# Four cross-attention layers on one core: probabilities transposed in two row tiles of 64 rows, two units a step, and the residual kept with features on the rows

## The chip, the cores and the metric

The kernel runs on one NeuronCore of a Trainium2 chip, one program with one launch. The metric is the device time of an execution in microseconds, the median of several runs. The profile is one further execution, recorded instruction by instruction. PE is TensorE (its weight loads are listed apart as PEld), DVE is VectorE, ACT is ScalarE, POOL is GpSimd, SP is SyncE, which issues the DMAs.

## What is computed

A batch of 128 sequences of 64 tokens with 128 features goes through four cross-attention layers against one context of 128 x 64 tokens with 256 features. Everything is float32. Layer 0 has 16 heads of width 64, a bias on some score columns, and a bias `bo`; layers 1 to 3 have an RMS norm ahead of the queries, 16 query heads and 4 key heads of width 8.

```python
# layer 0
q = x @ Wq;  k = ctx @ Wk;  v = ctx @ Wv            # 16 heads of 64
probs = softmax(q k^T / 8 + col_bias)
x = (probs v) @ Wo + bo + x
# layers 1, 2, 3
xn = x * rsqrt(mean(x*x) + eps) * norm_w
q = xn @ wq;  k = cond @ wk;  v = cond @ wv         # 16 query heads, 4 key heads of 8
x = x + (softmax(q k^T / sqrt(8)) v) @ wo
```

## The kernel before

The 128 sequences are cut into 32 groups g of four (T = 256 tokens). For every group the same list of *steps* is done, each named by kind, group, layer l and number u. On PE they are:

- `k` (4 steps, L694), `v` (6, L706), `k3` (L713): keys and values of all layers from the context; `q0` (4, L721): queries of layer 0.
- `s`: scores, in tiles of the PE array: layer 0 in tiles of 64 rows x 64 columns (L732), layers 1 to 3 in tiles of 32 rows x 64 columns (L743).
- `t` (L753): the probabilities of a *unit* transposed. A unit is an array `E` of 128 x 512: two sequences of 64 tokens on the 128 rows, eight heads of 64 keys along them. Each layer of a group has 4 units. One `t` step transposes one unit in four whole 128x128 pieces.
- `pv0` (L762, tiles of 64x64) and `pv` (L790, tiles of 128 rows x 32 columns): probabilities times values. `wo0` (L771) and `wo` (L796): output projection. `xt` (L665): the residual, kept with tokens on the rows (`xN`), is transposed to features on the rows (`xT`), from which `q` (L777) makes the queries of layers 1 to 3.

The softmax of a unit goes round the other engines: DVE takes the maximum and subtracts it (L954 and L958; layer 0 adds the bias and POOL subtracts), ACT exponentiates (L859, L852), DVE sums and inverts (L963, L966), POOL normalizes (L644), PE transposes, and ACT copies the result from PSUM back over `E` (`et`, L863). ACT also copies every other result of PE out of PSUM; DVE adds `wo0` and `wo` to the residual. PE results go through four PSUM banks in turn (`bank0` to `bank3`), the scores through four more. A step on PE waits until the previous user of its bank has been copied out.

The order of the steps on each engine is fixed by tables: each step has a time within a group's life, group g is moved by g x `PERIOD`, and every engine's queue is these times sorted. All engines wait for each other through semaphores. Four groups are thus under way at a time, in different layers. The last groups (28 to 31) have times of their own (`PE_ENDS` and so on), and the last two (`SPLIT`) do the steps of layers 1 to 3 and `wo0` in two halves of 128 tokens. `PE_FILL` puts 16 to 18 waits that are always fulfilled ahead of each `k` step on PE.

Of the kernel before, what the change touches and what calls it, by code (L numbers as in the profile page):

```python
# [40 lines left out]
PE_FILL = (18, 18, 16, 16)  # L41
PERIOD = 43.53
PE_TIME = {
    "k": {0: (30.28, 0, 14.31, 51.16)},
    "v": {0: (21.14, 37.8, 49.25, 36.09, 39.27, 41.84)},
    "k3": {0: (47.45,)},
    "q0": {0: (71.65, 69.92, 72.95, 66.36)},
    "s": {0: (76.07, 77.05), 1: (111.9,), 2: (143.36,), 3: (175.94,)},
    "t": {0: (94.04, 91.9, 96.41, 97.28),
          1: (130.16, 128.46, 122.67, 127.59),  # L50
          2: (159.58, 162.6, 158.28, 157.84),
          3: (194.83, 194.17, 193.73, 187.94)},
    "pv0": {0: (97.82, 98.8)},
    "wo0": {0: (103.09,)},
    "xt": {1: (107.55,), 2: (138.01,), 3: (169.65,)},
    "q": {1: (109.46,), 2: (140.38,), 3: (171.56,)},
    "pv": {1: (133.46,), 2: (165.14,), 3: (197.91,)},
    "wo": {1: (135.86,), 2: (167.94,), 3: (200.01,)},
}
ACT_TIME = {  # L60
    "k": {0: (34.56, 4.3, 18.1, 53.08)},
    "v": {0: (25.22, 39.25, 50.7, 37.55, 40.73, 44.78)},
    "k3": {0: (49.49,)},
    "q0": {0: (74.13, 70.98, 74.63, 70.11)},
    "exp": {0: (80.41, 85.19, 87.75, 85.75),
            1: (120.19, 118.66, 116.45, 120.9),
            2: (152.96, 153.95, 147.98, 149.19),
            3: (188.52, 182.87, 185.84, 180.45)},
    "et": {0: (95.03, 92.53, 97.11, 97.91),
           1: (130.79, 130.12, 123.35, 128.23),  # L70
           2: (160.7, 163.23, 159.03, 158.54),
           3: (195.63, 194.86, 194.37, 189.23)},
    "pv0": {0: (99.49, 100.47)},
    "x2": {1: (109.06,), 2: (141.94,), 3: (169.29,)},
    "xt": {1: (108.29,), 2: (139.06,), 3: (170.23,)},
    "q": {1: (110.14,), 2: (141.13,), 3: (173.37,)},
    "pv": {1: (134.61,), 2: (166.3,), 3: (199.06,)},
}
DVE_TIME = {
    "add": {0: (77.25, 81.06, 83.78, 79.49)},  # L80
    "max": {0: (78.14, 82.16, 84.55, 80.38),
            1: (113.05, 115.01, 114.34, 117.07),
            2: (145.86, 148.79, 144.51, 145.18),
            3: (181.14, 177.77, 182.49, 177.09)},
    "sum": {0: (86.87, 85.92, 88.83, 87.95),
            1: (126.36, 120, 117.74, 122.34),
            2: (153.84, 154.84, 149.47, 151.71),
            3: (190.07, 183.75, 186.72, 181.81)},
    "rcp": {0: (88.63, 86.67, 92.27, 92.07),
            1: (127.12, 121.47, 119.11, 123.71),  # L90
            2: (154.59, 157.26, 151.51, 153.54),
            3: (191.43, 185.32, 187.47, 184.43)},
    "wo0": {0: (106.87,)},
    "ssq": {1: (109.6,), 2: (142.68,), 3: (174.61,)},
    "sub": {1: (118.42, 116.38, 115.69, 119.31),
            2: (150.82, 152.38, 147.21, 148.1),
            3: (185.52, 180.45, 184.63, 178.44)},
    "wo": {1: (136.51,), 2: (168.81,), 3: (200.99,)},
}
POOL_TIME = {  # L100
    "xb": {0: (33.37,)},
    "sub": {0: (79.26, 82.91, 85.3, 81.5)},
    "nrm": {0: (89.03, 86.94, 92.55, 93.59),
            1: (127.48, 121.74, 119.39, 123.99),
            2: (155.66, 157.53, 151.78, 154.61),
            3: (191.71, 187.69, 188.74, 184.7)},
    "ms": {1: (110.08,), 2: (143.16,), 3: (175.09,)},
}
SP_TIME = {
    "cT": {0: (116.06,)},  # L110
    "kr": {1: (50.03,), 2: (73.03,), 3: (104.56,)},
    "lt": {0: (127.56,)},
    "xT": {0: (128.06,)},
    "st": {0: (202.62,)},
}

PE_ENDS = {
    28: {  # L120
        "s": {3: (172.75,)},
        "t": {2: (159.47, 159.47, 158.28, 157.84), 3: (187.48, 189.3, 186.49, 186.58)},
        "xt": {3: (168.97,)},
        "q": {3: (169.89,)},
        "pv": {2: (164.38,), 3: (190.31,)},
        "wo": {2: (164.61,), 3: (191.31,)},
    },
    29: {
        "s": {2: (142.53,), 3: (171.37,)},
        "t": {1: (128.31, 131.24, 129.24, 125.42),  # L130
              2: (159.07, 155.87, 157.44, 155.61),
              3: (218.3, 187.25, 190.66, 197.07)},
        "xt": {2: (135.25,), 3: (166.95,)},
        "q": {2: (137.77,), 3: (168.74,)},
        "pv": {1: (131.42,), 2: (163.31,), 3: (219.88,)},
        "wo": {1: (133.21,), 2: (165.67,), 3: (224.77,)},
    },
# [13 lines left out]
    },  # L151
# [891 lines left out]
```

## Time and profile before

| | |
|---|---|
| Runs | 1444.02, 1445.4, 1445.58 us; median 1445.4 |
| Span of the profiled execution | 1442.6 us (the runs are 1.4 to 3.0 us above it) |
| PE busy | 1416.4 us (98%), weight loads 1151.5 us |
| DVE, ACT, POOL busy | 1090.9, 1043.0, 787.3 us |
| Granted TensorE clock | full (2.4 GHz) in nearly every stretch |
| HBM | 20.68 MB read, 4.19 MB written |

A "busy" PE is one that has a matmul somewhere in its pipeline, so 98% says that it never stops, not that it streams data all the time. How long a step takes is therefore read from the start of one step to the start of the next. In the rows, `x4` counts machine instructions: a float32 matmul is two of them, a transpose is one.

### The profile page before, as it was taken

The numbers are of one execution on the slowest core, as the hardware profiler recorded it, in microseconds if no ns is written. First come the engines' busy times: TensorE is split into PE (matmuls) and PEld (weight loads), VectorE is DVE, ScalarE is ACT, GpSimd is POOL, SyncE is SP. The second block draws the span as 40 slices with busy tenths as digits, with TensorE's granted clock in tenths as the row PEclk, the third lists the DMA queues.
The fourth block names the chain that finished last, engine by engine and source line by source line (L and its number), as shares of the span: only waits on it lengthen the run. The fifth ranks groups of instructions, "written<-read, shape, count | busy, mean of one in ns | idle before, by whom it ended". The sixth has DMA issues, their size and how long they took to land.

```text
span 1442.6 us, 56878 instructions
## 1 busy us (share of the span) xinstructions
PE 1416.4 (98%) x23692; PEld 1151.5 (80%) x23692; DVE 1090.9 (76%) x2281; ACT 1043.0 (72%) x2321; POOL 787.3 (55%) x905
## 2 busy tenths in 40 slices
PE   8999999999999999999999999999999999999987
PEld 6778878888888888788888788888888887888765
DVE  1557777777777777777778777777777777777887
ACT  3567776777777777767777777777777777677777
POOL 3445555545555455555455555455554555554687
PEclk9999999999999999999999999999999999999999
DMA  5010111010111001111001110101110001110000
GB/s 157 21 28 18 29 29 30 24 29 18 30 29 31 23 18 29 30 29 30 24 19 29 29 30 24 29 19 29 29 32 23 23 25 30 29 28 18 18 7 14
DMA packets 58540, 41.16 MB, mean 29 GB/s; under 512 B 17456, under 2 KB 54064, under 8 KB 58288
## 3 DMA queue, kind: packets, MB, share of 16 engines
q1 hardware_dynamic: 57872, 37.19, 9.9%
q8 instruction: 192, 3.15, 0.9%
q14 instruction: 60, 0.49, 0.1%
q10 hardware_dynamic: 416, 0.33, 0.1%
HBM read 20.68 MB, written 4.19 MB: 17 GB/s over the span
## 4 chain that ended last, share of the span: by engine, by line
PE 96%; ACT 1%; DVE 1%; POOL 1%; issue 1%; DMA 0%
PE bank L706 17%; PE bank L694 16%; PE bank L753 16%; PE bank L771 8%; PE bank L721 7%; PE scores L743 7%; PE bank L790 7%; PE scores L732 5%; PE bank L762 5%; PE bank L796 3%; PE bank L777 3%; PE bank L713 2%; PE bank L665 1%; ACT E L863 1%; DVE st L954 0%
## 5 line engine op out<-in xcount | busy, mean ns | idle before, releaser
L644 POOL TENSOR_TENSOR E<-E,st 128x512 f32<-128x512 f32 x512 | 530.2, 1044 | 535.7 <-DVE st L966 535.5
L963 DVE TENSOR_REDUCE st<-E 128x8 f32<-128x512 f32 x512 | 344.7, 675 | 81.0 <-ACT E L859 40.0
L863 ACT COPY E<-bank 128x512 f32<-128x512 f32 x512 | 298.1, 598 | 96.7 <-PE bank L753 95.5
L859 ACT ACTIVATE E<-E,inv 128x512 f32<-128x512 f32 x384 | 278.5, 734 | 57.2 <-DVE E L958 56.7
L954 DVE TENSOR_REDUCE st<-scores 128x8 f32<-128x512 f32 x372 | 244.0, 683 | 97.0 <-PE scores L743 97.0
L753 PE MATMUL bank<-ident,E 128*128 128x128 f32 x2048 | 301.5, 276 | 0.9 <-POOL E L644 0.7
L753 PEld LDWEIGHTS bank<-ident,E 128*128 128x128 f32 x2048 | 241.5, 141 | 69.3 <-issue 28.2
L706 PE MATMUL bank<-wv,cT 128*128 128x374 f32 (+1 forms) x768 | 271.4, 478 | 0.0
L694 PE MATMUL bank<-cT,wk 128*128 128x256 f32 x1024 | 245.9, 384 | 7.0 <-issue 5.9
L958 DVE TENSOR_TENSOR E<-scores,st 128x512 f32<-128x512 f32 x372 | 245.9, 669 | 0.1
L694 PEld LDWEIGHTS bank<-cT,wk 128*128 128x128 f32 x1024 | 188.9, 192 | 32.1 <-issue 6.3
L706 PEld LDWEIGHTS bank<-wv,cT 128*128 128x128 f32 x768 | 132.1, 191 | 49.8
L640 POOL TENSOR_TENSOR E<-E,st 128x512 f32<-128x512 f32 x140 | 146.1, 1044 | 29.8 <-DVE st L948 26.0
L721 PE MATMUL bank<-xq,wq 128*128 128x256 f32 x512 | 131.0, 380 | 0.0
L820 ACT COPY V<-bank 128x374 f32<-128x374 f32 (+1 forms) x192 | 85.1, 443 | 50.7 <-PE bank L706 46.6
L771 PEld LDWEIGHTS bank<-wo,QT 128*128 128x128 f32 x1024 | 119.4, 192 | 2.1 <-ACT QT L868 0.3
L771 PE MATMUL bank<-wo,QT 128*128 128x128 f32 x1024 | 119.9, 275 | 0.1
L941 DVE TENSOR_TENSOR E<-scores,bias 128x512 f32<-128x512 f32 x128 | 86.2, 674 | 40.8 <-PE scores L732 40.8
L790 PEld LDWEIGHTS bank<-E,VB 128*32 128x32 f32 x6144 | 90.6, 110 | 28.6 <-issue 22.2
L743 PE MATMUL scores<-KB,QT 32*64 32x256 f32 x3072 | 110.1, 389 | 2.4 <-DVE E L958 1.5
L895 ACT COPY QT<-bank 128x256 f32<-128x256 f32 (+1 forms) x102 | 36.7, 360 | 102.0 <-PE bank L790 98.1
L790 PE MATMUL bank<-E,VB 128*32 128x64 f32 x6144 | 106.9, 221 | 3.2 <-ACT E L863 3.1
(58 smaller groups left out, 1627.0 us busy)
## 6 DMA issues: line engine op xcount, KB each, us to landing
KB<-K SPq DMA_DIRECT2D x1536, 8.0 KB
cT<-in_ctx_t SPq DMA_DIRECT2D x32, 256.0 KB, 2.8
xq<-in_x_t SPq DMA_DIRECT2D x32, 128.0 KB, 2.2
xin<-in_x SPq DMA_DIRECT2D x32, 128.0 KB, 2.3
out<-xN SPq DMA_DIRECT2D x30, 128.0 KB, 1.9
wk<-in_L_xattn_Wk SPq DMA_DIRECT2D x3, 256.0 KB, 5.5
wv<-in_L_xattn_Wv SPq DMA_DIRECT2D x2, 374.0 KB, 6.4
wq<-in_L_xattn_Wq SPq DMA_DIRECT2D x1, 512.0 KB, 6.2
```

The lines of the kernel that those rows point to most:

```text
L644: e.tensor_tensor(E3, E3, wide(stat[s][u][:, 16:24]), ALU.mult).then_inc(g_nrm.sem, 1)
L694: m = e.matmul(bank[:, T * jj:T * jj + T], wk0[:, k, 128 * j:128 * j + 128], cTg[:, k, :], start=(k == 0), stop=(k == 1))
L706: m = e.matmul(bank[:, 0:hi - lo], cTg[:, k, 128 * p:128 * p + 128], wv[:, k, lo:hi], start=(k == 0), stop=(k == 1))
L721: m = e.matmul(bank[:, T * jj:T * jj + T], wq0[:, 128 * j:128 * j + 128], xq[g % NX][:, :], start=True, stop=True)
L753: m = e.transpose(bank[:, 128 * k:128 * k + 128], E[s][u][:, 128 * k:128 * k + 128], ident[:, :])
L771: m = e.matmul(bank[:, 128 * p:128 * p + 128], QT[s][:, j, 128 * p:128 * p + 128], wo0[:, j, :], start=(j == 0), stop=(j == 7))
L790: m = e.matmul(bank[32 * r:32 * r + 32, 64 * b:64 * b + 64], VBg[:, b, c:c + 32], E[s][2 * (b // 2) + r // 2][:, n:n + 64], start=(gp == 0 ...
L859: e.activation(E[s][u][:, :], E[s][u][:, :], ACT.Exp, scale=inv[s][:, u // 2:u // 2 + 1]).then_inc(a_exp.sem, 1)
L863: e.copy(E[s][u][:, :], bank_of["t", g, l, u][:, :]).then_inc(a_et.sem, 1)
L954: e.tensor_reduce(stat[s][u][:, 0:8].rearrange("p (r h) -> p r h", r=2), scores_of[g, l, u], AX, ALU.max).then_inc(d_max.sem, 1)
L958: e.tensor_tensor(pairs(E[s][u][:, :]), scores_of[g, l, u], stat[s][u][:, 0:8].rearrange("p (r h a) -> p r h a", r=2, a=1).to_broadcast([1 ...
L963: e.tensor_reduce(stat[s][u][:, 8:16], heads(E[s][u][:, :]), AX, ALU.add).then_inc(d_sum.sem, 1)
```

## The change

**The transposes.** A `t` step now does two units (u = 0 or 1 stands for units 2u and 2u+1) and takes two banks. Each piece is the 64 rows of one sequence by 128 columns of `E` (two heads), transposed against a 64x64 identity into a 128x64 result. The upper and lower 64 rows go in turn, the upper to the first bank and the lower to the second, which is how the PE array is used as two row tiles. A unit was four instructions of 128 moving columns; it is eight of 64. `et` copies a whole bank as before; what lies where in `E` afterwards is different, and `pv0` and `pv` read it from there, with the same count of matmuls in the same tiles.

**The residual.** It is kept as `xT`, features on the rows. `wo0` and `wo` have the weights as the stationary operand and the 256 tokens as the moving one (half as many instructions of twice the columns). `xq`, the transposed input that `q0` reads, is also the residual's start: DVE adds `bo` (one number per row) and `xq` in one operation. `xN`, `xin`, their loads, the `bo` addition on POOL (`xb`), the `xt` transposes and their ACT copies are gone. The sum of squares needs tokens on the rows, so a step `x2` transposes `xT` (same size as `xt`), and ACT squares it out of PSUM. The output is stored transposed and turned back on the host; the next load of `xq` waits for `wo0`.

**The order.** All tables are new, `PERIOD` is 41.50 instead of 43.53, the tables of the last groups are empty, `SPLIT` is empty, `PE_FILL` is zero.

```diff
-PE_FILL = (18, 18, 16, 16)
-PERIOD = 43.53
+PE_FILL = (0, 0, 0, 0)
+PERIOD = 41.500813
...
-SPLIT = range(NG - 2, NG)
+SPLIT = range(NG, NG)
...
-            at = [(n + i) % 4 for i in range(2 if st[0] == "pv0" else 1)]
+            at = [(n + i) % 4 for i in range(2 if st[0] in ("pv0", "t") else 1)]
...
+                    w.wait_ge(d_ev, *[("wo0", g, 0, part(g, p)) for p in range(NP)])
                     e.dma_start(xq[g % NX][:, :], t["x_t"][g + NX]).then_inc(l_xq[g % NX].sem, 16)
...
-                    w.wait_ge(g_nrm, ("nrm", g, l, u))
-                    for k in range(4):
-                        m = e.transpose(bank[:, 128 * k:128 * k + 128], E[s][u][:, 128 * k:128 * k + 128], ident[:, :])
+                    w.wait_ge(g_nrm, ("nrm", g, l, 2 * u), ("nrm", g, l, 2 * u + 1))
+                    for r in range(2):
+                        for k in range(4):
+                            for i in range(2):
+                                rows, n = slice(64 * i, 64 * i + 64), 256 * r + 64 * k
+                                m = e.transpose(bank[i][:, n:n + 64], E[s][2 * u + r][rows, 128 * k:128 * k + 128],
+                                                ident[rows, rows])
                     m.then_inc(p_t.sem, 1)
...
-                    for p in halves(g, u):
-                        for j in range(8):
-                            m = e.matmul(bank[:, 128 * p:128 * p + 128], QT[s][:, j, 128 * p:128 * p + 128],
-                                         wo0[:, j, :], start=(j == 0), stop=(j == 7))
+                    for j in range(8):
+                        m = e.matmul(bank[:, tokens], wo0[:, j, :], QT[s][:, j, tokens], start=(j == 0), stop=(j == 7))
...
-                elif kind == "xt":
+                elif kind == "x2":
+                    w.wait_ge(l_ident, "ident")
                     w.wait_ge(d_ev, ("wo0" if l == 1 else "wo", g, l - 1, u))
                     for p in halves(g, u):
-                        to_rows(bank, 128 * p, xN[s][:, p, :], p == halves(g, u)[-1])
+                        m = e.transpose(bank[:, 128 * p:128 * p + 128], xT[s][:, 128 * p:128 * p + 128], ident[:, :])
+                    m.then_inc(p_ev.sem, 1)
...
                 elif kind == "et":
-                    w.wait_ge(p_t, ("t", g, l, u))
-                    e.copy(E[s][u][:, :], bank_of["t", g, l, u][:, :]).then_inc(a_et.sem, 1)
+                    w.wait_ge(p_t, ("t", g, l, u // 2))
+                    e.copy(E[s][u][:, :], bank_of["t", g, l, u // 2][u % 2][:, :]).then_inc(a_et.sem, 1)
...
-                    e.tensor_tensor(flat(xN[s])[:, tokens], bank[:, tokens], flat(xin[s])[:, tokens], ALU.add
-                                    ).then_inc(d_ev.sem, 1)
+                    e.scalar_tensor_tensor(xT[s][:, tokens], bank[:, tokens], bo[:, 0:1], xq[g % NX][:, tokens], ALU.add,
+                                           ALU.add).then_inc(d_ev.sem, 1)
```

What this does to PE's queue is seen at two places of a period in the middle of the program. The first is the stretch from the scores of layer 1 to the scores of layer 0. Before (`wos` is the weight of `wo`, `E_3` the fourth unit):

```order
L743 MATMUL scores<-KB_0,QT 64x256 x16
L796 MATMUL bank<-wos,QT 128x128 x2
L721 MATMUL bank<-xq,wq 128x256 x2
L753 MATMUL bank<-ident,E_3 128x128 x4
L753 MATMUL bank<-ident,E_2 128x128 x4
L721 MATMUL bank<-xq,wq 128x256 x2
L753 MATMUL bank<-ident,E_0 128x128 x4
L721 MATMUL bank<-xq,wq 128x256 x2
L694 MATMUL bank<-cT,wk 128x256 x4
L753 MATMUL bank<-ident,E_1 128x128 x4
L732 MATMUL scores<-KT,QT 64x64 x64
```

and now, at the same place (L476 are the scores of layer 1, L454 is `q0`, L427 `k`, L439 `v`, L489 `t`, L465 the scores of layer 0):

```order
L476 MATMUL scores<-KB_1,QT 64x256 x16
L454 MATMUL bank<-xq,wq 128x256 x2
L532 MATMUL bank<-QT,wos 128x256
L427 MATMUL bank<-cT,wk 128x256 x4
L454 MATMUL bank<-xq,wq 128x256 x6
L489 MATMUL bank<-ident,E_0 128x64 x8
L489 MATMUL bank<-ident,E_1 128x64 x8
L439 MATMUL bank<-wv,cT 128x374 x2
L489 MATMUL bank<-ident,E_2 128x64 x8
L489 MATMUL bank<-ident,E_3 128x64 x8
L465 MATMUL scores<-KT,QT 64x64 x64
```

The four transposes stood singly between whole-array matmuls, themselves whole-array work; now they stand in two pairs, each in the two-row-tile form, with a whole-array `v` between them. The second place is the end of a period, from the scores of layer 2 over `wo0` to the `q` of layer 1. Before:

```order
L743 MATMUL scores<-KB_1,QT 64x256 x16
L753 MATMUL bank<-ident,E_3 128x128 x4
L694 MATMUL bank<-cT,wk 128x256 x4
L771 MATMUL bank<-wo,QT 128x128 x16
L753 MATMUL bank<-ident,E_2 128x128 x4
L753 MATMUL bank<-ident,E_1 128x128 x4
L665 MATMUL bank<-ident,xN 128x128 x2
L753 MATMUL bank<-ident,E_0 128x128 x4
L706 MATMUL bank<-wv,cT 128x374 x2
L777 MATMUL bank<-xT,wqs 128x256
```

and now (L507 is `wo0`, L512 `q`, L518 the new `x2`):

```order
L476 MATMUL scores<-KB_1,QT 64x256 x16
L489 MATMUL bank<-ident,E_2 128x64 x8
L489 MATMUL bank<-ident,E_3 128x64 x8
L507 MATMUL bank<-QT,wo 128x256 x8
L489 MATMUL bank<-ident,E_0 128x64 x8
L489 MATMUL bank<-ident,E_1 128x64 x8
L439 MATMUL bank<-wv,cT 128x374 x2
L512 MATMUL bank<-xT,wqs 128x256
L518 MATMUL bank<-ident,xT 128x128 x2
```

The `k` step between the `pv0` steps and `wo0` is gone from there, `wo0` is enclosed by two transposing pairs, and `q` no longer waits for a transpose and its copy.

## Rows read from the trace of the kernel before

**Rows 1.** The page, busy time of each engine and share of the span.

```profile
PE 1416.4 (98%) x23692; PEld 1151.5 (80%) x23692; DVE 1090.9 (76%) x2281; ACT 1043.0 (72%) x2321; POOL 787.3 (55%) x905
```

**Rows 2.** The page, the chain that ended last, by engine.

```profile
PE 96%; ACT 1%; DVE 1%; POOL 1%; issue 1%; DMA 0%
```

**Rows 3.** Timeline of PE, the `wo0` steps of groups 3, 18, 29 and 31.

```profile
176.95 3.73 PE L771 MATMUL bank<-wo,QT 128*128 128x128 f32 x32
...
834.19 3.73 PE L771 MATMUL bank<-wo,QT 128*128 128x128 f32 x32
...
1316.17 3.73 PE L771 MATMUL bank<-wo,QT 128*128 128x128 f32 x32
...
1384.87 1.95 PE L771 MATMUL bank<-wo,QT 128*128 128x128 f32 x16
```

**Rows 4.** Busy time by windows: 14 periods, and the end.

```profile
220.80:834.20 613.40, 612.69 (x10362) 501.09 (x10361) 478.92 (x995) 450.22 (x994) 333.12 (x378) 1.00 0.10 27
...
1384.90:1442.60 57.70, 44.87 (x836) 33.19 (x834) 44.84 (x102) 46.21 (x116) 43.75 (x56) 0.97 0.04 12
```

Columns: window, its length, then busy us and instructions of PE, PEld, DVE, ACT, POOL, then granted clock, DMA share and GB/s.

**Rows 5.** Timeline of PE in a middle period: start, length, line, operation, array tile, count.

```profile
804.67 1.89 PE L694 MATMUL bank<-cT,wk 128*128 128x256 f32 x8
806.40 0.60 PE L753 MATMUL bank<-ident,E 128*128 128x128 f32 x4
806.93 2.10 PE L732 MATMUL scores<-KT,QT 64*64 64x64 f32 x128
808.96 1.10 PE L790 MATMUL bank<-E,VB 128*32 128x64 f32 x64
809.99 0.66 PE L753 MATMUL bank<-ident,E 128*128 128x128 f32 x4
810.48 1.42 PE L706 MATMUL bank<-wv,cT 128*128 128x374 f32 x4
...
817.92 1.89 PE L694 MATMUL bank<-cT,wk 128*128 128x256 f32 x8
819.74 1.12 PE L743 MATMUL scores<-KB,QT 32*64 32x256 f32 x32
820.79 1.10 PE L790 MATMUL bank<-E,VB 128*32 128x64 f32 x64
821.82 1.10 PE L713 MATMUL bank<-cT,wks 128*96 128x256 f32 x4
822.76 0.60 PE L753 MATMUL bank<-ident,E 128*128 128x128 f32 x4
823.20 0.61 PE L796 MATMUL bank<-wos,QT 128*128 128x128 f32 x4
```

**Rows 6.** Weight loads of tile `bank` by line: ns min/median/max, first and last start.

```profile
L790 PEld LDWEIGHTS bank<-E,VB x6144: 106/110/110, 77.2 to 1438.1; 128*32 128x32 f32 x199
L762 PEld LDWEIGHTS bank<-E,V x4096: 129/135/135, 48.0 to 1387.6; 64*64 64x64 f32 x196
L753 PEld LDWEIGHTS bank<-ident,E x2048: 137/141/230, 43.0 to 1436.5; 128*128 128x128 f32 x187
L694 PEld LDWEIGHTS bank<-cT,wk x1024: 186/190/337, 5.9 to 1365.4; 128*128 128x128 f32 x171
```

**Rows 7.** The page, costliest groups: busy us, mean ns of one, idle before.

```profile
L644 POOL TENSOR_TENSOR E<-E,st 128x512 f32<-128x512 f32 x512 | 530.2, 1044 | 535.7 <-DVE st L966 535.5
...
L753 PE MATMUL bank<-ident,E 128*128 128x128 f32 x2048 | 301.5, 276 | 0.9 <-POOL E L644 0.7
L863 ACT COPY E<-bank 128x512 f32<-128x512 f32 x512 | 298.1, 598 | 96.7 <-PE bank L753 95.5
...
L790 PE MATMUL bank<-E,VB 128*32 128x64 f32 x6144 | 106.9, 221 | 3.2 <-ACT E L863 3.1
```

**Rows 8.** Timeline of PE, the step ahead of the first `wo0`.

```profile
50.56 1.97 PE L694 MATMUL bank<-cT,wk 128*128 128x256 f32 x8 [0.46 <-ACT QT L868]
```

More of the change, by code:

```diff
@@ L73 @@
[L73 to L77, printed above, removed]
+    "k": {0: (3.68386, -15.27201, -6.17337, 31.67261)},
+    "v": {0: (1.38578, 7.02085, 22.92723, 7.72795, 7.45838, 19.83981)},
+    "k3": {0: (20.92541,)},
+    "q0": {0: (46.49501, 45.92059, 43.6006, 46.83102)},
+    "exp": {0: (53.45354, 53.85427, 64.05064, 60.19724),
+            1: (89.26426, 87.38091, 88.31216, 89.8139),
+            2: (119.0247, 119.99253, 120.41612, 125.81305),
+            3: (157.12044, 158.35286, 146.78456, 148.29428)},
@@ L78 @@
+    "et": {0: (72.80188, 70.12283, 74.38432, 74.91003),
+           1: (94.37576, 97.20368, 92.87151, 93.63442),
+           2: (130.02138, 130.69038, 130.95683, 130.76886),
+           3: (163.36371, 165.90794, 161.03983, 161.0276)},
+    "pv0": {0: (77.48236, 77.47354)},
+    "x2": {1: (84.45866,), 2: (118.43633,), 3: (137.54581,)},
+    "q": {1: (83.49375,), 2: (115.56548,), 3: (133.12088,)},
+    "pv": {1: (104.57246,), 2: (131.76498,), 3: (167.77863,)},
 }
 DVE_TIME = {
-    "add": {0: (77.25, 81.06, 83.78, 79.49)},
@@ L81 @@
[L81 to L98, printed above, removed]
+    "add": {0: (55.2541, 53.04177, 57.80328, 56.50077)},
+    "max": {0: (55.53031, 55.83358, 59.00545, 58.41666),
+            1: (87.28643, 84.47971, 84.43642, 89.53838),
+            2: (118.07358, 118.40023, 119.44369, 120.23959),
+            3: (152.51299, 148.31429, 145.74995, 142.83961)},
@@ new lines @@
+    "sum": {0: (60.32318, 64.11482, 68.19706, 64.69957),
+            1: (93.38689, 90.42387, 92.61554, 94.70716),
+            2: (123.99953, 123.33926, 124.87226, 125.45511),
+            3: (155.08859, 158.66318, 155.26501, 154.11835)},
+    "rcp": {0: (61.15165, 64.66232, 68.84377, 65.42065),
+            1: (94.25659, 92.98835, 94.45288, 95.94984),
+            2: (125.00317, 124.44888, 125.29739, 126.52991),
+            3: (156.56917, 160.68649, 158.46443, 154.92969)},
+    "wo0": {0: (81.3189,)},
@@ L360 @@
-SPLIT = range(NG - 2, NG)
-ON_ACT = ("q0", "pv0", "xt", "q", "pv", "k", "v", "k3")
+}
+SPLIT = range(NG, NG)
+ON_ACT = ("q0", "pv0", "x2", "q", "pv", "k", "v", "k3")
 ON_DVE = ("wo0", "wo")
@@ L505, in xattn_kernel @@
         for st in of(PE_ORDER, *ON_ACT, *ON_DVE, "t"):
-            at = [(n + i) % 4 for i in range(2 if st[0] == "pv0" else 1)]
+            at = [(n + i) % 4 for i in range(2 if st[0] in ("pv0", "t") else 1)]
             n += len(at)
             before[st] = [held[i] for i in at if held[i]]
-            bank_of[st] = [banks[i] for i in at] if st[0] == "pv0" else banks[at[0]]
-            for i in at:
-                held[i] = st
+            bank_of[st] = [banks[i] for i in at] if st[0] in ("pv0", "t") else banks[at[0]]
+            for j, i in enumerate(at):
+                held[i] = ("et", *st[1:3], 2 * st[3] + j) if st[0] == "t" else st
         l_ident = signal("l_ident", ["ident"], 16)
@@ L591, in sync_program @@
                 s = g % NS
-                if kind == "xT" and g + NS < NG:
-                    w.wait_ge(d_ev, ("wo0", g, 0, 0))
-                    e.dma_start(xin[s][:, :, :], x_r[g + NS]).then_inc(l_x[s].sem, 16)
-                elif kind == "cT" and g + NC < NG:
+                tokens = slice(128 * halves(g, u)[0], 128 * halves(g, u)[-1] + 128)
+                if kind == "cT" and g + NC < NG:
                     w.wait_ge(p_ev, ("k3", g, 0, 0), *[("k", g, 0, i) for i in range(4)], *[("v", g, 0, i) for i in range(6)])
@@ L794, in tensor_program @@
                     w.wait_ge(a_ev, ("pv", g, l, u))
-                    for p in halves(g, u):
-                        m = e.matmul(bank[:, 128 * p:128 * p + 128], QT[s][:, 1, 128 * p:128 * p + 128],
-                                     wos[:, l - 1, :], start=True, stop=True)
+                    m = e.matmul(bank[:, tokens], wos[:, l - 1, :], QT[s][:, 1, tokens], start=True, stop=True)
                     m.then_inc(p_ev.sem, 1)
```

326 lines of the change are left out of this document (53 added, 273 removed), and 55 rows, old and new, of tables (ACT_ENDS, PE_ENDS).

## The prediction, made before the changed kernel ran

> **What bounds the kernel now.** I read the busy times first: PE 98%, its weight loads 80%, DVE 76% [rows 1]. Then the chain that ended last: 96% of it is PE [rows 2]. Then the places of `wo0`, to see the rhythm: group 3 at 176.95, group 18 at 834.19, so 657.24 / 15 = 43.82 us a group; group 29 at 1316.17 is 26 such periods after group 3 to within 0.1 [rows 3]. In 14 of these periods PE is busy 612.69 of 613.40 us, DVE 478.92, that is 34.2 a period [rows 4]. So the span is 177 of start, 26 periods that PE's queue sets, and 126.4 from group 29's `wo0` to the end. A step's price is its share of PE's queue: start to start.
>
> **What a step costs on PE** [rows 5]. `k`, 8 instructions of 256 columns, takes 1.73 (804.67 to 806.40): 0.216 each. `t` takes 0.44 (822.76 to 823.20): 0.110 for 128 columns. `wo0`, 32 of 128 columns, would by this be 3.5; it stands at about 3.6 with its tail (length 3.73, [rows 3]). Tiled steps work in rounds, one matmul in each tile. Layer-0 scores: 128 in four tiles, 32 rounds, 2.03. `pv`: 64 in four tiles, 16 rounds, 1.03. The matmul's own length falls from 276 for 128 columns to 221 for 64 [rows 7], 0.86 ns a column, so a round of 64 columns streams 0.055; 16 of them are 0.88 and 32 are 1.76. The rest, 0.15 and 0.27, is the price of changing the shape of the array, plus a few ns a round.
>
> Three readings isolate that price. `k` ahead of scores takes 1.82 (817.92 to 819.74) instead of 1.73: **0.09** on leaving. A first whole-array step after tiled work is longer: `k3` 0.94 (821.82 to 822.76) instead of 4 x 0.216, **0.08**; `t` 0.49 (809.99 to 810.48) instead of 0.44, **0.05**. That second part goes with the first weight load, which nothing hides: loads last 110 for 32 columns, 135 for 64, 190 for 128, about 0.85 ns a column, but only 141 for the 128 columns of a transpose [rows 6], some 0.055 of streaming against 0.109. So entering a whole-array matmul costs 0.09 + 0.10 or so, 0.20 with rounding up; entering a transpose 0.09 + 0.055, 0.15.
>
> **The change, per period.**
>
> *The transposes.* 64 instructions x 0.110 = 7.0 become 128 of 64 columns in two tiles, 64 rounds. No row has this form. The lower bound of a round is the streaming 0.055, as in `pv`; the layer-0 scores (2.03 / 32 = 0.063 with their change of shape in it, about 0.058 without) are the nearest with two row tiles. I take 0.056: 3.6. **-3.4**. The upper bound is that the tiles do not overlap, 0.110 a round, no gain at all.
>
> *Changes of shape.* Before, a period had 12; the transposes were whole-array work like their neighbours. Now they are a shape of their own. From the order: seven blocks of them (t3.0, t2.0, t2.1, t1, t0.0, t0.1, t3.1; only layer 1's pairs stand together), so 7 x 0.15 = 1.05 to enter; and the whole array is entered nine times (eight matmuls, one `x2`: 8 x 0.20 + 0.15 = 1.75) instead of four (`wo`, `k3` and two `t`: 0.20 + 0.17 + 2 x 0.15 = 0.67). The eight entries to scores, `pv` and `pv0` stay. **+2.1**. Bounds: 0, if two row tiles switch for nothing, and 12 x 0.20 = 2.4.
>
> *wo0 and wo.* 16 x 0.216 = 3.46 for about 3.57, and 3 x 0.43 for 3 x 0.44. **-0.1**. *xt to x2*: same matmuls, 0. *The fills*: PE has no idle time that they could explain in the middle [rows 4]; 0, at most 0.2 gained.
>
> Sum -3.4 + 2.1 - 0.1 = **-1.4 us**: a period of 42.4.
>
> Two rules of the Trainium skill bear on this; the sum above does without them. TensorEngine Tiling (Properties) says that changing the tiling mode, not just the tile, drains the engine; the trace agrees, with 0.09 on each change. TensorE: Matmul & The Clock Gate (LDWEIGHTS) gives a weight load as columns / 1.2 ns whatever the number of rows. It speaks against this change: 64 rows do not halve the load, a round would be limited by a 128-column load of 107 ns, and by the page the transposes would still cost 64 x 0.107 = 6.8. The trace's plain loads agree with it in slope; the transposes' load is shorter by 0.05 [rows 6], so I side with the row.
>
> **What hides the rest.** DVE needs 34.2 of the 42.4 us, 81% [rows 4]; the 1.1 us less of copies on ACT and the POOL addition are off the path and give nothing. `wo0` waits for two `pv0` steps' copies, four of about 0.64, 2.6 from the first's end; it is covered by the second `pv0` (1.0), scores (1.05 and a change) and a pair of transposes (0.6), so just. If that cover is short, PE loses tenths a period. A `t` now waits for two units normalized instead of one, 1.044 on POOL later [rows 7], and fills two of the four banks in 0.6 where ACT needs 2 x 0.598 to empty them [rows 7]. Mostly 1.3 to 1.7 of whole-array work stands behind it, so I price this at 0 and keep it as a rival. The later load of `xq` has two periods to land: 0. SP's queue stands behind that wait, but its next entries are due later: 0.
>
> **Start and end.** Start: half-filled periods save some 2 us up to group 3; the first `wo0` had `k` ahead of it and still waited 0.46 for the copy [rows 8], and without it waits some 1.7 more. Together 0; within 2.
>
> End: without the split, each layer of the last group is one serial chain. From group 29's `wo0`: (a) one period without the `k` of group 32, 42.4 - 1.7 = 40.7. (b) The next has no `k`, `v`, `k3`: PE would need 27, but DVE still has four softmaxes, 34.2. Each hangs in a chain, so I take 37. (c) From group 31's `wo0`, five and a half layers of softmax at 34.2 / 4 = 8.55, 47 of DVE; then two places where nothing else is left to fill: between layers 2 and 3 of group 31, and behind the last. From the last inverse: one or two normalizations at 1.044, `t` 0.6, two `et` 1.2, `pv` 1.1, copy 0.4, `wo` 0.6, add 0.4, `q` 0.6, copy 0.4, scores 1.1, about 7.5. Twice that is 15, and the start of this stretch and the store 4: 66. Sum 143.7 instead of 126.4: **+17**. Before, this last stretch took 57.7 with PE busy only 44.87 and DVE 44.84 of it [rows 4]. I give the sum 8 either way.
>
> **Sum.** 177 + 26 x 42.4 + 143.7 = 1423.1, say 1423.5 against the profiled 1442.6: -19. The profiled execution's span lies 2.8 under the median 1445.4; with that carried over, **1426 us**, 1.3% faster.
>
> **Rivals.**
>
> 1. *The forecast*: rounds overlap, changes of shape eat 60% of the gain. 1410 to 1442. 0.50.
> 2. *Changes of shape are cheap for two row tiles* (a whole-height array split in two might not drain). For: `k3`, 96 columns, changes shape for nothing. Against: every other tiled step pays 0.09 [rows 5]. Without them a period is 40.3, 28 periods x 2.1 less: 1367; with half, 1396. 0.24.
> 3. *The change doesn't do what it says*: two row tiles do not overlap, because the 128-column load sets the pace. For: the number of loads doubles and each is as wide as before; no row shows two such loads side by side. Against: `pv0` and scores in 64x64 tiles load and stream in two row tiles at once. T stays at 7.0, the period becomes 45.8: 1426 + 29 x 3.4 = 1525. Slower than before once a round takes over 0.085. 0.12.
> 4. *Banks and pairs*: transposes overlap, but PE waits at its seven blocks for ACT to empty two banks, or for the second unit. Where an `et` is late by one copy, 0.6, at three of the seven, that is 1.8 a period x 26: 1473. It decides against the change from 0.75 us a period. For: ACT already waits for PE rather than the reverse [rows 7], so there is slack; against it, PE's steps got shorter and the copies did not. 0.10.
>
> 0.04 is left for a mixture that ends within 0.2% (3 us, what a measurement of this kernel can tell from no change). Range for 8 in 10: all of 1, the upper half of 2, the lower part of 4: 1386 to 1452. Faster: 0.50 + 0.24 + a part of 4, less the tail of 1: 0.78. Same 0.04, slower 0.18.
>
> **What would show it.** Between two `wo0` in the middle 42.4 us. A pair `t` to the next step 0.6 (0.45 of rounds, 0.15 to enter), against 0.5 if rival 2 holds and 1.0 if 3 does; the next `v` longer than 1.26 + 0.09 by 0.1. PE's idle before `t` and `wo0` still near nothing; if ACT's `et` stands there with over 0.5 us a period, rival 4. DVE at some 81% in the middle. From group 29's `wo0` to the end 144. The forecast is wrong if the round isn't 0.056, if the change of shape has another price for this tile, or if the end, for which there is no row of an unsplit group alone, takes over 155.

## The result and the profile after

The changed kernel takes **1469.8 us** (median of 4 runs, 1464.1 to 1472.4) against 1444.7 for the kernel before (4 runs): ratio 1.0169, interval 1.0146 to 1.0193. It is slower, by 1.7%; 1426 was forecast, and the range ended at 1452. The profiled execution took 1467.5, with a span of 1465.7.

The page of the changed kernel, span and busy time of each engine, beside [rows 1]:

```profile
span 1465.7 us, 58100 instructions
...
PE 1395.2 (95%) x25024; PEld 1064.8 (73%) x25024; DVE 1088.6 (74%) x2291; ACT 998.0 (68%) x2177; POOL 748.9 (51%) x849
```

PE is busy 21 us less than before in a span that is 23 us longer: 44 us more of idle time have come in. Where they lie is seen by windows: a stretch of the middle as long as fourteen periods, and two stretches at the end (columns as in [rows 4]).

```profile
220.00:834.00 614.00, 601.87 (x10948) 460.57 (x10948) 474.00 (x995) 434.29 (x953) 322.92 (x365) 1.00 0.09 24
1310.60:1392.80 82.20, 70.67 (x1490) 53.85 (x1488) 67.17 (x143) 55.01 (x115) 46.01 (x52) 0.96 0.08 18
1392.80:1465.70 72.90, 42.48 (x736) 29.74 (x732) 42.41 (x92) 30.55 (x58) 24.80 (x29) 0.63 0.03 9
```

In the middle PE is idle 12 of 614 us, where it was idle 0.7 of 613 [rows 4]; in the last 73 us it is idle 30, at a mean granted clock of 0.63. The timeline gives the rhythm, again by the places of `wo0` (now L507), first four in the middle (groups 18 to 21), then those of groups 29 to 31:

```profile
832.33 3.72 PE L507 MATMUL bank<-QT,wo 128*128 128x256 f32 x16
875.58 3.72 PE L507 MATMUL bank<-QT,wo 128*128 128x256 f32 x16
919.12 3.72 PE L507 MATMUL bank<-QT,wo 128*128 128x256 f32 x16
961.66 3.72 PE L507 MATMUL bank<-QT,wo 128*128 128x256 f32 x16
...
1310.56 3.72 PE L507 MATMUL bank<-QT,wo 128*128 128x256 f32 x16
1354.59 3.72 PE L507 MATMUL bank<-QT,wo 128*128 128x256 f32 x16
1392.84 3.72 PE L507 MATMUL bank<-QT,wo 128*128 128x256 f32 x16
```

The periods are 43.25, 43.54, 42.54: the last comes within 0.14 of the forecast 42.4, but they are not alike, while before all were 43.8 [rows 3]. Group 3's `wo0` stands at 175.4, so 26 periods took 1310.56 - 175.4 = 1135.2, 43.66 on the mean. Against before: the start -1.5 us, the middle -4 (forecast -37), the end 155.1 instead of 126.4, +28.7 (forecast +17). -1.5 - 4 + 28.7 = 23, the difference of the spans.

What PE waited for, by total (columns: the line that waited, what ended the wait, us in total, times, the longest), for the changed kernel:

```profile
PE bank L489 <- POOL E L383: 17.7, 9, 8.9
PE bank L527 <- issue: 12.4, 14, 1.3
...
PE scores L476 <- issue: 4.7, 9, 1.3
PE scores L465 <- issue: 4.1, 8, 0.8
```

The first row lies in the end of the program, but for 0.3. The three with "issue", 21.2 us together, are idle time for which the profile shows nothing to wait for, and they stand *inside* a step. The timeline of PE shows one:

```profile
801.21 0.71 PE L489 MATMUL bank<-ident,E 64*128 64x64 f32 x16
801.85 1.52 PE L439 MATMUL bank<-wv,cT 128*128 128x374 f32 x4
803.31 0.71 PE L489 MATMUL bank<-ident,E 64*128 64x64 f32 x16
803.94 2.10 PE L465 MATMUL scores<-KT,QT 64*64 64x64 f32 x128
805.97 0.65 PE L527 MATMUL bank<-E,VB 128*32 128x64 f32 x30
807.95 0.72 PE L527 MATMUL bank<-E,VB 128*32 128x64 f32 x34 [1.34 <-issue]
```

`pv` halts for 1.34 us after 30 of its 64 matmuls, though all its inputs are there. Counting PE's instructions in the trace (weight loads, matmuls, semaphore waits) from the first, each such halt in the middle stands behind number 192 or 193 modulo 256. The places 256 instructions apart are called *limits* of the blocks below. And among the DMA queues of the page there is one that carries instructions (packets, MB, share); here it is for the changed kernel, and for the kernel before:

```profile
q8 instruction: 197, 3.23, 0.9%
```

```profile
q8 instruction: 192, 3.15, 0.9%
```

3.23 MB in 197 packets are 16.4 KB each, and PE's 2 x 25024 loads and matmuls with some 500 waits, divided by 197, are about 256 to a packet. Hence the theory: **PE's instructions arrive in blocks of 256, and a block that is used up too fast leaves PE waiting for the next.** The layer-0 scores use 256 instructions in 2.03 us, and `pv` of layer 2 another 128 in 1.03 right behind them.
The records of the single packets tie the two together. The halt above ends 1.3 us after a packet of that queue has landed, and so does every other: the 136 halts of over 0.4 us between 170 and 1440 us in the changed kernel and in four of the kernels below (b_nofill, b_shift, h_bad, f_whole) all stand at a limit, and each ends 1.2 to 1.6 us after a packet landed, with a median of 1.4; of all times in h_bad, only some 6% lie that far behind a landing. A packet takes 0.9 to 1.5 us.

The Trainium skill describes the mechanism (Runtime: NRT & Kernel Launch, Instruction fetch mechanics): a FIFO for each engine that is refilled in blocks of 256 instructions over a DMA queue of its own; the 16.4 KB packets of some 256 instructions agree. The Trainium skill adds there that the fetch is hidden since the sequencer issues slower than blocks arrive; the halts measured here, 0.4 to 1.3 us each in the changed kernel, say that this doesn't hold for PE with small tiled matmuls.

### The profile page after: what moved, and what is told of

Same layout as the page of the kernel before. It is cut to its first block, busy times and chain, and to the rows that moved or that the text cites. A ratio compares the mean times of both kernels' runs of the same rounds, so it can differ in the third digit from the quotient of the medians.

```text
span 1465.7 us, 58100 instructions
## 1 busy us (share of the span) xinstructions
PE 1395.2 (95%) x25024; PEld 1064.8 (73%) x25024; DVE 1088.6 (74%) x2291; ACT 998.0 (68%) x2177; POOL 748.9 (51%) x849
## 3 DMA queue, kind: packets, MB, share of 16 engines
q8 instruction: 197, 3.23, 0.9%
## 4 chain that ended last, share of the span: by engine, by line
PE 90%; DVE 3%; issue 2%; ACT 2%; POOL 1%; SPq 1%; DMA 0%; POOLq 0%; DVEq 0%; ACTq 0%
PE bank L439 17%; PE bank L427 15%; PE bank L489 11%; PE bank L454 8%; PE bank L507 7%; PE scores L476 7%; PE bank L527 7%; PE scores L465 5%; PE bank L499 4%; PE bank L532 3%; PE bank L512 3%; PE bank L446 2%; PE bank L518 2%; DVE st L680 1%; DVE E L684 1%
## 5 line engine op out<-in xcount | busy, mean ns | idle before, releaser
L383 POOL TENSOR_TENSOR E<-E,st 128x512 f32<-128x512 f32 x512 | 527.8, 1042 | 371.7 <-DVE st L692 369.4
L599 ACT COPY E<-bank 128x512 f32<-128x512 f32 x512 | 274.0, 589 | 29.1 <-PE bank L489 27.3
L439 PE MATMUL bank<-wv,cT 128*128 128x374 f32 (+1 forms) x768 | 283.9, 493 | 0.4 <-issue 0.4
L684 DVE TENSOR_TENSOR E<-scores,st 128x512 f32<-128x512 f32 x384 | 255.4, 679 | 2.2
L427 PE MATMUL bank<-cT,wk 128*128 128x256 f32 x1024 | 250.2, 388 | 4.7 <-DMA wk<-in_L_xattn_Wk 4.7
L489 PEld LDWEIGHTS bank<-ident,E 64*128 64x128 f32 x4096 | 150.7, 141 | 102.1 <-issue 70.6
L427 PEld LDWEIGHTS bank<-cT,wk 128*128 128x128 f32 x1024 | 191.2, 191 | 33.2 <-issue 4.6
L489 PE MATMUL bank<-ident,E 64*128 64x64 f32 x4096 | 182.0, 232 | 19.4 <-POOL E L383 17.7
L439 PEld LDWEIGHTS bank<-wv,cT 128*128 128x128 f32 x768 | 133.9, 189 | 61.0 <-issue 0.7
L379 POOL TENSOR_TENSOR E<-E,st 128x512 f32<-128x512 f32 x128 | 129.5, 1043 | 87.8 <-DVE st L674 87.8
L395 POOL TENSOR_TENSOR nt<-nt,powers 128x2 f32<-128x2 f32 x96 | 18.7, 195 | 240.5 <-DVE nt L711 240.5
L548 ACT COPY KT<-bank 128x512 f32<-128x512 f32 x128 | 75.0, 586 | 82.2 <-PE bank L427 82.2
L454 PE MATMUL bank<-xq,wq 128*128 128x256 f32 x512 | 124.2, 385 | 0.0
L476 PE MATMUL scores<-KB,QT 32*64 32x256 f32 x3072 | 115.5, 396 | 6.6 <-issue 4.7
L507 PE MATMUL bank<-QT,wo 128*128 128x256 f32 x512 | 119.0, 386 | 1.3 <-ACT QT L604 1.3
L580 ACT ACTIVATE QT<-bank 128x512 f32<-128x512 f32 x128 | 75.7, 592 | 61.3 <-PE bank L532 56.5
```

Of the source, the lines that this page charges most:

```text
L383: e.tensor_tensor(E3, E3, wide(stat[s][u][:, 16:24]), ALU.mult).then_inc(g_nrm.sem, 1)
L427: m = e.matmul(bank[:, T * jj:T * jj + T], wk0[:, k, 128 * j:128 * j + 128], cTg[:, k, :], start=(k == 0), stop=(k == 1))
L439: m = e.matmul(bank[:, 0:hi - lo], cTg[:, k, 128 * p:128 * p + 128], wv[:, k, lo:hi], start=(k == 0), stop=(k == 1))
L454: m = e.matmul(bank[:, T * jj:T * jj + T], wq0[:, 128 * j:128 * j + 128], xq[g % NX][:, :], start=True, stop=True)
L489: m = e.transpose(bank[i][:, n:n + 64], E[s][2 * u + r][rows, 128 * k:128 * k + 128], ident[rows, rows])
L507: m = e.matmul(bank[:, tokens], wo0[:, j, :], QT[s][:, j, tokens], start=(j == 0), stop=(j == 7))
```

## The experiments

Each kernel ran on one chip beside runs of the kernel before; times are medians, with the ratio to that kernel and its interval. Kernels from different chips are compared by these ratios.

**1. b_nofill: the kernel before without its fills.**

```diff
-PE_FILL = (18, 18, 16, 16)
+PE_FILL = (0, 0, 0, 0)
```

> The kernel before with PE_FILL set to (0, 0, 0, 0) and nothing else: 68 waits that are always met already go from each group, 34 of TensorE's instructions, so that a group has 1502 of them instead of 1536 = 6 x 256. Theory of the instruction blocks: TensorE's instructions come in blocks of 256, and a block that begins late in the long run of small matmuls of s of layer 0 and pv of layer 2 is not there in time; with 1502 a group the places where the blocks begin wander over the group, and now and then one falls there. Periods between 43.7 and 45, not constant, 0.5 to 1.2 us more a group on the mean, 1458 to 1475 us. Rival, the waits are padding without use: 1443 to 1447 us, periods constant at 43.8. Rival, they cost their 0.106 us an instruction: 3.6 us a group less, down to 1350 us.

1483.7 us, ratio 1.0279 (1.0247 to 1.0311). To take away 68 waits a group that never wait costs 40 us. The mean period is 45.35 and the single ones go from 43.75 to 48.2; those without a halt are 43.75, so the 34 instructions themselves cost 0.07 us. The effect is larger than the 1458 to 1475 expected. Six halts of 1.4 to 2.5 us, 11.8 in total, lie in `pv0`, while halts were expected in the layer-0 scores and `pv` alone:

```profile
309.62 0.68 PE L762 MATMUL bank<-E,V 64*64 64x64 f32 x28 [2.54 <-issue]
```

In these six the packet itself starts late: 1.8 to 6.1 us after the last limit, 1.0 to 1.8 us after `pv0` has begun; for the halts elsewhere in this kernel it is 0.2 to 1.7 us after the limit. PE goes on 1.2 to 1.5 us after it has landed, as everywhere. What makes a packet start late was not tested.

Both rivals fall.

**2. b_shift: the kernel before, its blocks moved.** Waits on a load that is long done, in the first three groups alone:

```diff
-                    for _ in range(PE_FILL[u]):
+                    for _ in range(PE_FILL[u] + (EARLY if g < 3 else 0)):
...
+                    for _ in range(V_FILL + (EARLY if g < 3 else 0)):
+                        e.wait_ge(l_wk[1].sem, 16)
```

with `EARLY = 7`, `V_FILL = 0`.

> The kernel before with 7 more met waits at each k and v step of the first three groups alone (some 105 instructions in the first 140 us, where TensorE waits for loads anyway), and nothing else. Every group after them is the same as before, with 1536 instructions. Theory of the instruction blocks: the blocks now begin at other places, one of them 337 instructions into the run of s of layer 0 and pv of layer 2 (it was 184 in, and the next after the run), in every group: each period 44.6 to 45.8 us instead of 43.82, all alike, 1465 to 1500 us. Rival, the place of an instruction in its block has no effect: periods 43.8, 1445 to 1452 us with what the waits at the start may cost.

1512.6 us, ratio 1.0473 (1.0455 to 1.049), the slowest kernel here and above the 1465 to 1500 expected, though from the fourth group on it is the kernel before, instruction for instruction. The mean period is 46.40 us. What PE waited for, by total:

```profile
PE bank L794 <- issue: 31.1, 28, 1.6
PE bank L696 <- issue: 16.8, 29, 6.0
PE bank L757 <- issue: 13.0, 22, 1.0
```

A halt of 1.1 in `pv` (L794) in each group was expected. That a group loses 2.6 us and not 0.8 to 2 has two reasons above all: another limit falls behind `pv0` and `s`, into a transpose (L757, up to 1.0, 13.0 in total), and the fills of the `k` step that follows (L696) now lie open, some 0.4 us each time, where before they hid behind queued matmuls. The three rows, without the one wait of 6.0, make 2.0 of the 2.6; the rest is not itemised.

**3. h_align and h_bad: the changed kernel, its blocks fixed in a good and in a bad place.** Three of the eight pairs are transposed on the whole array again, 16 instructions less each; with 4 for the fills a group has 1580 - 48 + 4 = 1536.

```diff
-PE_FILL = (0, 0, 0, 0)
+PE_FILL = (2, 2, 2, 2)
+EARLY = 9
...
+WHOLE = {(0, 1), (2, 0), (0, 0)}
...
+                            if (l, u) in WHOLE:
+                                m = e.transpose(bank[r][:, 128 * k:128 * k + 128],
+                                                E[s][2 * u + r][:, 128 * k:128 * k + 128], ident[:, :])
+                                continue
```

`pv0` and `pv` read E for these pairs where the kernel before has it. h_bad differs by `EARLY = 13` alone.

> The changed kernel with whole-array transposes for three of its eight transpose steps (both of layer 0 and the first pair of layer 2, those that stand alone between whole-array steps), two met waits at each k step and nine more at each k and v step of the first three groups: 1536 instructions a group, with the blocks' beginnings where the changed kernel was fastest (phase 136 of 256 at wo0). Theory of the instruction blocks: periods constant at 42.5 to 42.9 us with no issue idle inside pv, 1436 to 1448 us (26 times 1.0 less than the changed kernel's mean of 43.66; its end stays near 155 us). Rival, the row tiles themselves or contention make the long periods: they stay at 43.4 or more and vary, 1462 us or more.

> h_align with thirteen instead of nine extra waits at the k and v steps of the first three groups, and nothing else: the steady groups are the same instruction for instruction, at phase 196 of 256, so that a block begins 377 instructions into the run of s of layer 0 and pv of layer 2. Theory of the instruction blocks: periods constant at 43.8 to 45 us, 1470 to 1500 us. Rival, the row tiles or contention: the same as h_align within 3 us.

h_align: **1436.4** us, ratio 0.9941 (0.992 to 0.9962). h_bad: **1487.9**, ratio 1.0303 (1.0288 to 1.0319). One number, which acts in the first three groups alone, is worth 51 us. Both lie in the ranges of the theory. From group 2 to group 28 every period of h_align is 42.64 or 42.65; here are three of its `wo0`:

```profile
855.50 3.72 PE L519 MATMUL bank<-QT,wo 128*128 128x256 f32 x16
898.14 3.72 PE L519 MATMUL bank<-QT,wo 128*128 128x256 f32 x16
940.78 3.72 PE L519 MATMUL bank<-QT,wo 128*128 128x256 f32 x16
```

h_bad's run from 43.8 to 45.2, 44.55 on the mean; they were expected to be constant. The same place of the group in the timeline, h_align first:

```profile
787.28 2.10 PE L470 MATMUL scores<-KT,QT 64*64 64x64 f32 x128
789.30 1.10 PE L542 MATMUL bank<-E,VB 128*32 128x64 f32 x64
790.34 1.52 PE L444 MATMUL bank<-wv,cT 128*128 128x374 f32 x4
```

and h_bad:

```profile
819.02 2.10 PE L470 MATMUL scores<-KT,QT 64*64 64x64 f32 x128
821.05 1.09 PE L542 MATMUL bank<-E,VB 128*32 128x64 f32 x61
823.38 0.30 PE L542 MATMUL bank<-E,VB 128*32 128x64 f32 x3 [1.25 <-issue]
823.62 1.52 PE L444 MATMUL bank<-wv,cT 128*128 128x374 f32 x4
```

And what h_bad waited for, by total:

```profile
PE bank L542 <- issue: 30.5, 29, 1.7
...
PE bank L498 <- issue: 10.4, 24, 0.9
```

30.5 + 10.4 = 41 of the 51 us are named. The rest is not itemised, but the rows above show a part of it: from the `scores` to the `v` behind them h_bad takes 4.60 us and h_align 3.06, that is 1.54 more with a halt of 1.25, so 0.3 more comes in beside each such halt; the three matmuls behind the halt take 0.24 (823.38 to 823.62), where 64 of them take 1.04 otherwise. The packets fit: in h_bad one is under way from 820.82 to 821.94, and PE goes on at 823.38. Since the two kernels have the same steady instructions, the rival (tiles or contention) is out.

All blocks of the steady part of seven kernels (f_whole is experiment 4), worked out from the records: by the time in which PE used up a block, how many there are, and the median and largest gap at its end, in us.

```
block used in   < 2.3 us        2.3 to 2.8      2.8 to 3.5      3.5 to 5        > 5 us
before          -               -               -               -               169: 0.11 0.22
after           27: 0.92 1.55    5: 0.31 1.11    3: 0.31 0.86   13: 0.04 0.97   126: 0.04 0.41
h_align         -               -               -               -               169: 0.05 0.31
h_bad           29: 1.19 1.89   28: 0.58 1.13   -               -               113: 0.04 0.17
f_whole         28: 0.69 1.77   -               -                4: 0.21 0.21   126: 0.04 0.72
b_shift         56: 1.00 1.79   -               -               -               113: 0.03 0.04
b_nofill        22: 1.20 1.86    5: 0.31 1.86    4: 1.26 2.35    8: 0.26 2.15   126: 0.04 2.76
```

A block used in 2.0 us is followed by a gap of about 1, one used in 2.5 by 0.6, and above 5 there is hardly any but in b_nofill. So the next block takes about 3 us to come, as a rule: 0.8 or so until its packet starts, 1.1 for the packet, 1.4 until PE goes on. Where the packet starts later, as in the `pv0` of b_nofill, a block that was used more slowly is followed by a halt too.

**4. f_whole: all transposes on the whole array, nothing else undone.**

```diff
+WHOLE = {(0, 1), (2, 1), (0, 0), (3, 1), (1, 1), (2, 0), (3, 0), (1, 0)}
```

> The changed kernel with all eight transpose steps of a group on the whole array (the probabilities then lie in E as before, and pv0 and pv read them there); pairs of units, order, end and everything else as in the changed kernel. 1452 instructions a group, so the blocks' beginnings wander; the periods whose wo0 stands at 140 to 165 of 256 should be free of their waits and give the pure price. Theory that the row tiles pay only where tiled steps are neighbours: 43.5 to 43.8 us there, 1.0 to 1.2 above the changed kernel's best 42.54. Rival, the tiles save 0.24 us at each of 8 places (forecast of 32 columns of time less a step): 44.4 or more. Second rival, the changes of shape eat all of it: 42.6.

1488.7 us (one run). 1452 instructions a group; the blocks wander, the mean period is 44.57. The periods without a halt are 43.63 to 43.64, eight of them, as the theory had it; the rivals, 44.4 and 42.6, are out. Here is one:

```profile
800.18 3.62 PE L515 MATMUL bank<-QT,wo 128*128 128x256 f32 x16
843.82 3.62 PE L515 MATMUL bank<-QT,wo 128*128 128x256 f32 x16
```

So the row tiles are worth 43.63 - 42.54 = **1.09 us** a group. In h_align three pairs without them cost only 42.64 - 42.54 = 0.10 (with its four fills in it); the other five bring 0.99. A pair in row tiles takes 0.64 (801.21 to 801.85) and on the whole array 0.87:

```profile
803.64 1.04 PE L489 MATMUL bank<-ident,E 128*128 128x128 f32 x8
804.51 1.42 PE L440 MATMUL bank<-wv,cT 128*128 128x374 f32 x4
805.77 0.59 PE L520 MATMUL bank<-xT,wqs 128*128 128x256 f32 x2
```

but the `v` behind it takes 1.26 here (804.51 to 805.77) and 1.46 behind the tiled one (801.85 to 803.31). So a tiled pair that stands alone between whole-array steps gains 0.23 and loses 0.20 again; the 0.99 of the other five, 0.20 each, says that next to another tiled step a pair keeps most of its gain.

**5. b_nosplit: the kernel before with the end of the changed one.** `PE_ENDS` to `SP_ENDS` empty, and

```diff
-SPLIT = range(NG - 2, NG)
+SPLIT = range(NG, NG)
```

> The kernel before without its tables for the last groups (PE_ENDS to SP_ENDS empty) and without the split of the last two (SPLIT empty), nothing else; the groups up to wo0 of group 28 keep their order, their 1536 instructions and their blocks. Theory that the split and the tables of the last groups carried the end: from wo0 of group 29 to the end 148 to 158 us instead of 126.4, and with the three periods ahead of it unchanged 1466 to 1476 us. Rival, the longer end of the changed kernel is of its deeper order (124 us from wo0 to the last wo of a group, 97 before): then leaving out the split alone costs 3 to 10 us, 1448 to 1455 us.

1463.8 us, ratio 1.0138 (1.0121 to 1.0155). `wo0` of group 29 stands at 1316.4, the span ends at 1460.9: 144.5 instead of 126.4. That is +18, somewhat under the 148 to 158 of the first theory and far over the rival. So of the +28.7 us at the changed kernel's end, some 18 come from the split and the tables of the last groups, if these are worth as much there as in the kernel before.

**6. h_warm: matmuls on constants where PE idles in the last two groups.**

```diff
+                warm = {"t": 3, "pv": 3, "wo": 1, "q": 1}.get(kind, 0) if g >= 30 and l else 0
+                if kind == "t" and warm:
+                    first = [x for x in PE_ORDER if x[:3] == (kind, g, l)][0]
+                    warm = 0 if st != first else 18 if (g, l) == (31, 3) else 3
+                for _ in range(warm):
+                    e.matmul((bank[0] if kind == "t" else bank)[:, 0:256], wo0[:, 0, :], wk0[:, 0, 0:256],
+                             start=True, stop=True)
```

> h_align, with matmuls of 256 columns on constants (their result is overwritten) where TensorE waits for its input in the layers 1 to 3 of the last two groups: 3 ahead of the first t and of pv of each layer, 1 ahead of q and wo, 18 ahead of the first t of the last layer; 0.43 us each at full clock, about what TensorE idles there. Theory that the granted clock of half speed lengthens the end: the clock stays at 1.0 to the end, the steps of the chain that took 1.9 to 2.0 us at half clock (s, pv) take 1.1, and the end of 147.4 us from wo0 of group 29 falls by 4 to 7 us, 1429 to 1433. Rival, the end is the chain of VectorE, ScalarE and GpSimd, and the added work is in the way: no change or up to 5 us more.

1433.8 us, ratio 0.9934 (0.9917 to 0.995): not to be told from h_align's 0.9941, though the theory expected 1429 to 1433. The last rows of PE in h_align, at the lower of the two clock levels (granted 0.50 there):

```profile
1419.52 2.21 PE L498 MATMUL bank<-ident,E 64*128 64x64 f32 x32 [8.90 <-POOL E L386]
1422.98 1.94 PE L542 MATMUL bank<-E,VB 128*32 128x64 f32 x64 [1.25 <-ACT E L614]
1425.39 1.22 PE L547 MATMUL bank<-QT,wos 128*128 128x256 f32 x2 [0.48 <-ACT QT L636]
```

In h_warm the same `pv` takes 1.10 and `wo` 0.70, the clock is 1.0. But from group 29 to the end it is 148.6 instead of 147.4 in the profiled executions: what the clock gives, the added matmuls may take. The test bounds nothing but their sum. The runs of the changed kernel itself go from 1464.1 at a mean clock of 0.983 to 1472.4 at 0.974, which speaks for some us of the clock; how many was not settled.

**7. h_end, h_end2, h_end3: h_align with the last two groups split again.** The steps from the last groups on stand in a list for each engine (a line of it shown), worked out with the durations of these traces.

```diff
-SPLIT = range(NG, NG)
+SPLIT = range(NG - 2, NG)
...
+    order += [(k, int(g), int(l), int(u)) for k, g, l, u in (st.split(".") for st in LAST[engine].split())]
```

> h_align with the last two groups split into their two pairs again (SPLIT as in the kernel before, which the changed code still supports) and, from wo0 of group 29 on, a list of steps for each engine that was worked out offline for it (from the order of the kernel before and measured durations). All groups up to there as in h_align. Theory that the end of the changed kernel is long because its last groups are not split and go on in the order of the steady state: from wo0 of group 29 to the end 124 to 131 us instead of 147.4, 1413 to 1420 us. Rival, the end is set by what the three last groups must do on VectorE and TensorE whatever the order: 142 us or more, 1430 us or more.

1427.0 us, ratio 0.988 (0.9865 to 0.9894); the end is 141.4, neither theory's. One wait shows what was missed:

```profile
PE bank L609 <- DVE xT L798: 12.5, 1, 12.5
```

The addition of `wo0` of group 29 overwrites `xT` and needs the store of group 26; `q` (L609) waits for it. In the timeline of SP's queue:

```profile
1249.85 48.87 SPq L442 DMA_DIRECT2D KB<-K  x72
1298.76 0.44 SPq L446 DMA_DIRECT2D out<-xT  x1
1299.25 11.01 SPq L442 DMA_DIRECT2D KB<-K  x16
```

The 16 transfers of one layer's KB hold the queue 11 us, far more than the order had reckoned with. The store stood behind 72 of them.

> As h_end (h_align with the last two groups split and a worked-out order at the end), but the order, now from wo0 of group 28 on, reckons with the 10.9 us that SyncE's queue takes for one layer's 16 transfers of KB, so that no store of a group, and no wo0 that reuses its xT, stands behind several of them. Theory that h_end lost its gain in that one wait of 12.5 us and in the clock behind it: from wo0 of group 29 to the end about 125 to 132 us, 1412 to 1419 us. Rival, the chain of the split groups is longer than reckoned: 138 us or more, 1425 us or more.

> As h_end2, another order of about the same reckoned length (1.4 us longer), which begins only at wo0 of group 29. Both theories: within 4 us of h_end2.

h_end2 **1414.5** us, ratio 0.9786 (0.9773 to 0.9799), from group 29 to the end 126.6; h_end3 1414.6, ratio 0.9791 (0.9778 to 0.9805), 121.3, with 7 us more ahead of it, since its list holds back `wo0` of group 29 (h_end2 holds back group 28's in the same way): the totals count here. These beat both kernels, by 30 us and by 55, but they are other kernels than the changed one: blocks fixed in place, three pairs on the whole array, and an end of its own.

## Why the prediction was wrong, step by step

- **The rhythm.** "A step's price is its share of PE's queue", with a middle of 26 equal periods. This is the step that failed. It holds only while the queue is fed: a group's count of instructions modulo 256 and the phase at which it begins decide whether PE runs out of instructions. Mean 43.66 against 42.54 without halts: 1.12 x 26 = 29 us, where the forecast put the idle time of the middle at nothing.
- **The fills.** "PE has no idle time that they could explain in the middle", so "0, at most 0.2 gained". Their own price was right, 0.07 (43.82 to 43.75). What they did, bringing a group to 1536, was not seen. It could have been: 740 loads, 740 matmuls and 56 waits a group can be counted ahead of any run, and the instruction queue's packets stand on the page.
- **The transposes, -3.4, and the changes of shape, +2.1.** Net -1.3 forecast, -1.09 measured (f_whole against the changed kernel). The pair in 0.64 is the forecast 0.6, the exit of 0.2 into a whole-array step too. The Trainium skill's rule on weight loads that was weighed there (TensorE: Matmul & The Clock Gate, LDWEIGHTS), by which the forecast estimated a round of 107 ns, would have made a pair 8 x 0.107 = 0.86 by that estimate, before any change of shape, which is the whole array's 0.87. With 0.64, change of shape included, the row was right to be followed.
- **wo0 and wo, -0.1.** With all that isn't tiling 43.82 became 43.63, -0.19.
- **Period 42.4.** 42.54 in its best periods. That much of the forecast came as worked out.
- **The rivals.** 2 (cheap changes) would be 40.3, 3 (no overlap) 45.8 us; neither came. 4 (banks) gives nearly the measured total, 1473, but by a mechanism that isn't there: h_align has the same pairs and banks, and PE is busy 614.00 of 614 us in its middle; and in the changed kernel the halts stand mostly inside `pv` and the scores, while rival 4 would put them ahead of a transpose. None of the rivals was the right one. The threshold given under rival 3, a round of 0.085, doesn't follow from the sums: by them a period gains nothing once a round takes (7.0 + 0.1 - 2.1) / 64 = 0.078.
- **The end, +17.** It is +28.7: (a) 44.0 for 40.7, (b) 38.3 for 37, (c) 72.9 for 66. 18 of it are the split and the tables (b_nosplit). In h_align, the same order with its blocks in place, the end is 147.4, so some 8 more belong to halts, to the less favourable blocks and, in an unknown part, to the clock; the last 3 are left for the changed order itself. This split is an estimate: the profiled execution of h_align, 1431.1, is the fastest of its four, 5 us under their median. The forecast's mark for being wrong, over 155, was just reached.
- **The start, 0.** It came 1.5 us earlier, within the 2 that were allowed. The 0.46 of [rows 8] was misread: that wait is `k`'s, not `wo0`'s.

Had every period of the middle been the best one, 1465.7 - 29 = 1437 would have been the span, 6 below before's: still a gain, but a third of the forecast one, because the end stays long. h_align's span is 1429, with a shorter end as well.

## What to carry to other kernels

Count an engine's instructions between two repeats of a long unrolled loop, modulo the size of an instruction block (here 256), ahead of an edit that adds or drops some: an edit of the count moves every later limit, and waits that are always met and look like waste may be there to keep the count. Where a dense stretch uses a block faster than the next one comes (2 us against 3 here), put the limit near the middle of the stretch, so that half of it is used up from a block that has long been there, and make the loop a multiple of the block so that it stays there; look for "issue" idle inside a step in the timeline, since no semaphore points to it, and set the landings of the instruction packets beside it. Tile steps that stand next to other tiled ones; alone between whole-array steps the changes of shape took back 0.20 of 0.23 here.

## What the runs showed that was not expected

- Two kernels whose steady groups are the same, instruction for instruction, differ by 51 us (1436.4 and 1487.9) through 4 more waits at each of the `k` and `v` steps of the first three groups; and the kernel before falls from 1443.6 to 1512.6 by such a shift.
- PE can use a block of its instructions about 1.4 us after its packet has landed, as a rule 3 us after the block ahead of it began to be used: halts of about 1.0 behind blocks used in 2.0 us, 0.6 behind 2.5, none as a rule above 5. In b_nofill some packets started late, and halts of up to 2.5 followed slower blocks; what delays a packet stays open.
- SP's queue was held 11.0 us by the 16 transfers of KB of one layer, and 48.9 by 72 of them, 0.68 each (h_end).
